# Scaling h by its root mean square on ScalarE, ahead of the last FFN block, in place of VectorE

## The chip, the cores and the metric

The kernel runs on one core of one Trainium2 chip. The metric is the device time of one execution in microseconds. Three executions of the kernel before took 677.26, 679.06 and 679.69 us; their median is 679.06. The profiled execution took 677.59 us.

## What is computed

The input x has the shape (2, 2048, 256), fp32. With `xn` the layer norm of x, the reference is

```
h   = xn + cosformer_attn(rmsnorm(xn, norm1_w))        # 16 heads, linear attention, cos and sin parts
m   = gelu(rmsnorm(h, norm2_w) @ mlp_w1 + mlp_b1) @ mlp_w2 + mlp_b2
ffn = bitlinear(relu(bitlinear(xn, w_fc) + gate * (xn @ v.T @ fast_b.T @ u.T)) ** 2, w_proj)
out = x + (h + m) + ffn
rmsnorm(h, w) = h * rsqrt(mean(h * h) + 1e-6) * w
```

The attention is causal and is written with running sums of k and v. The hidden width of both feed-forward parts is 1024. The change is about `rmsnorm(h, norm2_w)`: the multiplication of h by `rsqrt(mean(h * h) + 1e-6)`. The weight `norm2_w` is folded into `mlp_w1` when the kernel sets up.

## The kernel before

The 4096 tokens are taken in 8 tiles of 512 tokens (four blocks of 128, two of each batch). Tile 0 and tile 7 are written out, tiles 1 to 6 run in a loop. There is no planner: every engine has its own instruction stream, written by hand in the order in which it executes, and the streams meet in semaphores only. A waiting instruction holds everything that stands behind it on its engine.

In a tile TensorE does the attention of the four blocks, between them the FFN part in eight hidden blocks of 128 (`ffn_up(m)`, `ffn_down(m)`), then the output projection, then the MLP in eight hidden blocks (`mlp_up(m)`, `mlp_down(m)`) between which the transposes and the q and k products of the next tile lie. Matrix products are done in fp32r with a high and a low part, so that for every hidden block ScalarE makes the activation and a high part and VectorE the low part (`split`, L908).

The stretch of the change lies between the output projection and the MLP:

- TensorE: output projection (L1289) into two PSUM banks, `ffn_down(5)`, `ffn_up(7)` (L1143 and L1148), `ffn_down(6)` (L1158), then for each block k a wait for `hs_done` and two transposes of `xs` (L1301), then the first half of `mlp_up(0)` (L1315), which waits for `cT_hi`, then `ffn_down(7)`.
- VectorE: two adds that make h (`ctxn`, L980), `split(6)`, the scaling of the four blocks of h by `r2` into `xs` (L985), `split(7)`, then the low part of the transposed h (`cT_lo`, L990), and the read-out of the FFN sums (L996).
- ScalarE: `ffn_block(6)`, four Squares of h with a running sum (L702), which write the squares themselves into `xs` as waste, `ffn_block(7)` (Relu L646, Square L649, copy L651), the high part of the transposed h (`cT_hi`, L707), the scaling of the next tile's x into `xs` (L587), and the MLP's Gelu passes (L656, L659).
- GpSimd: for each half of the blocks an add (L531) and a pow with -0.5 (L533) that make `r2` from the sums; then `res = xb + ctxn` (L537), which waits for `split(7)`.

`hs_done` counts the scaled blocks; its waiter is TensorE at L1301. SP issues the DMAs and is not touched.

Of the kernel before, what the change touches and what calls it, by code (L numbers as in the profile page):

```python
# [31 lines left out]
ALU = mybir.AluOpType  # L32
ACT = mybir.ActivationFunctionType
# [4 lines left out]
NB = 4  # L38
# [42 lines left out]
def program(nc, x, qkv_w, qkv_b, out_w, out_b, norm1_w, norm2_w, mlp_w1, mlp_b1, mlp_w2, mlp_b2,  # L81
            fast_b, w_fc, w_proj, u, v, gate, consts, trig, out):
    with ExitStack() as ctx:
        def sb(name, shape, dt=F32):
            return ctx.enter_context(nc.sbuf_tensor(name, shape, dt))

        def sem(name):
            return ctx.enter_context(nc.semaphore(name))
# [28 lines left out]
        xs = sb("xs", [P, NB, E])  # L117
# [3 lines left out]
        ctxn = late[:, 1, :, :]  # L121
# [80 lines left out]
        r2 = sb("r2", [P, NB])  # L202
# [73 lines left out]
        r2_done = sem("r2_done")  # L276
        hs_done = sem("hs_done")
# [16 lines left out]
        def full_use(t, n):  # L294

            return 2 * KE + t * N_FULL + n

        def ffn_place(m):

            return m + min(max(m - 1, 0), NB)  # L300

        def ffn_use(t, m):
            return dense_use(t, ffn_place(m))
# [7 lines left out]
        def mlp_use(t, m, more):  # L311
            return dense_use(t, NB + mlp_place(m, more))

        def mlp_full(t, m, more):
            return full_use(t, mlp_place(m, more))
# [13 lines left out]
        def shared_use(t, n):  # L329

            return KE + t * N_SHARED + n

        def later(eng, sem_, n):

            if not isinstance(n, int) or n > 0:
                eng.wait_ge(sem_, n)

        def chunk_block(j):

            return (j % B) * 2 + j // B  # L340
# [215 lines left out]
        def _(act):  # L556
            def z_hi(t):

                act.wait_ge(upd_full, t * N_UPD + 1)
                act.activation(z_st[:, :], upd_ps[:, :], ACT.Copy).then_inc(z_hi_done, 1)  # L560
# [5 lines left out]
            def w1_hi_half(k):  # L566

                act.wait_ge(in_w1[k], 16)
                act.activation(raw_w1[k], raw_w1[k], ACT.Copy, scale=n2w[:, k:k + 1]).then_inc(w1_hi_done, 1)
                act.wait_ge(w1_hi_done, 2 * k + 1)  # L570
                act.activation(w1_hi[:, k, :], raw_w1[k], ACT.Copy).then_inc(w1_hi_done, 1)
# [11 lines left out]
            def scale_x(t):  # L583
                act.wait_ge(ln_pow, t * 8 + 7)
                act.wait_ge(x_in, t * 32 + 32)
                for k in range(NB):
                    act.activation(xs[:, k, :], xin[:, k, :], ACT.Identity, scale=xs_scale[:, k:k + 1],  # L587
                                   bias=xs_bias[:, k:k + 1]).then_inc(xs_done, 1)

            def x_hi(t):  # L590
                for m in range(KE):
                    act.wait_ge(shared_full, shared_use(t, m - KE) + 1)
                    act.activation(xT_hi[:, m, :], shared[m][:, :], ACT.Copy).then_inc(xT_hi_done, 1)

            def relu_kq(t):

                if not isinstance(t, int) or t:
                    act.wait_ge(q_trig_done, t * 2 * NB)
                for i, (dst, base) in enumerate(((kT, KE), (qT, 0))):
                    for m in range(KE):  # L600
                        act.wait_ge(dense_full, kq_full(t, i * KE + m) + 1)
                        act.activation(dst[:, m, :], dense[m][:, :], ACT.Relu,
                                       bias=qkb[:, base + m:base + m + 1]).then_inc(dense_free, 1)
# [37 lines left out]
            def body(t, more):  # L641
                def ffn_block(m):

                    act.wait_ge(dense_full, full_use(t, m) + 1)
                    later(act, wide_used, t * 2 * HB + max(m - 1, 0))
                    act.activation(wide[:, m % 2, :], dense[ffn_place(m) % 2][:, :], ACT.Relu,  # L646
                                   scale=scales[:, m:m + 1]).then_inc(dense_free, 1)
                    act.wait_ge(dense_free, ffn_use(t, m) + 1)
                    act.activation(wide[:, m % 2, :], wide[:, m % 2, :], ACT.Square).then_inc(wide_done, 1)  # L649
                    act.wait_ge(wide_done, t * HB + m + 1)  # L650
                    act.activation(wide_hi[:, m % 2, :], wide[:, m % 2, :], ACT.Copy).then_inc(hi_done, 1)  # L651

                def mlp_block(m):
                    act.wait_ge(dense_full, mlp_full(t, m, more) + 1)
                    act.wait_ge(wide_used, t * 2 * HB + HB + m - 1)
                    act.activation(wide[:, m % 2, :], dense[m % 2][:, :], ACT.Gelu_apprx_tanh,  # L656
                                   bias=b1[:, m:m + 1]).then_inc(dense_free, 1)
                    act.wait_ge(dense_free, mlp_use(t, m, more) + 1)
                    act.activation(wide_hi[:, m % 2, :], wide[:, m % 2, :], ACT.Copy).then_inc(hi_done, 1)  # L659

                def trig_v(j):

                    k = chunk_block(j)
                    act.wait_ge(shared_free, shared_use(t, S_V + k // 2) + 1)
                    later(act, upd_full, t * N_UPD + max(2 * j - 1, 0))
                    for r in range(2):
                        c = 2 * POS + 2 * r + k % 2
                        act.activation(v_trig[:, j % 2, :, r, :],
                                       v_tok[:, k, :, :].rearrange("p (m h) e -> p m (h e)", m=KE),
                                       ACT.Copy, scale=tab[:, c:c + 1]).then_inc(v_trig_done, 1)  # L670

                act.wait_ge(tab_in, t * 16 + 16)
                act.wait_ge(q_lo_stacked, (t + 1) * N_Q_LO * 16)
                trig_v(0)
                ffn_block(0)

                for g in range(2):
                    act.wait_ge(k_turned, t * 2 + g + 1)
                    act.activation(k_tok[:, 2 * g:2 * g + 2, :].rearrange("p b n -> p (b n)"), accum[g][:, :],
                                   ACT.Copy).then_inc(k_tok_done, 1)  # L680
                ffn_block(1)
                if isinstance(t, int) and t == 0:
                    w1_hi_half(1)
                def read_context(j):

                    act.wait_ge(av_done, (t * NB + j + 1) * 4)
                    later(act, ctx_full, t * NB + j)
                    act.activation(ctxT[:, :], dense[0][:, :], ACT.Copy).then_inc(dense_free, 1)  # L688

                for j in range(NB):  # L690
                    if j + 1 < NB:
                        trig_v(j + 1)
                    read_context(j)
                    ffn_block(j + 2)
                for m in range(KE):
                    act.wait_ge(shared_full, shared_use(t, S_CT + m) + 1)
                    act.activation(cT_hi[:, m, :], shared[m][:, :], ACT.Copy).then_inc(cT_hi_done, 1)
                ffn_block(6)
                for k in range(NB):

                    act.wait_ge(shared_free, shared_use(t, S_OUT + k // 2) + 1)
                    act.activation(xs[:, k, :], ctxn[:, k, :], ACT.Square, scale=float(E) ** -0.5,  # L702
                                   accum_out=mean_sq[:, k:k + 1]).then_inc(ssq_done, 1)
                ffn_block(7)
                for m in range(KE):
                    act.wait_ge(shared_full, shared_use(t, S_HT + m) + 1)
                    act.activation(cT_hi[:, m, :], shared[m][:, :], ACT.Copy).then_inc(cT_hi_done, 1)  # L707
                if more:
                    scale_x(t + 1)
                for m in range(HB):  # L710
                    mlp_block(m)
                    if m == 0 and more:
                        x_hi(t + 1)
                    if m == MLP_BEFORE_KQ - 1 and more:
                        relu_kq(t + 1)
                if more:
                    z_hi(t + 1)

            body(0, True)
            with act.Fori(1, NT - 1) as t:  # L720
                body(t, True)
            body(NT - 1, False)


        @block.vector
        def _(dve):
# [177 lines left out]
            def body(t, more):  # L904
# [75 lines left out]
                    dve.tensor_tensor(ctxn[:, 2 * g:2 * g + 2, :].rearrange("p b n -> p (b n)"), shared[g][:, :],  # L980
                                      xn[:, 2 * g:2 * g + 2, :].rearrange("p b n -> p (b n)"), ALU.add).then_inc(shared_free, 1)
                split(6)
                for k in range(NB):
                    dve.wait_ge(r2_done, t * 4 + k // 2 * 2 + 2)
                    dve.tensor_scalar(xs[:, k, :], ctxn[:, k, :], r2[:, k:k + 1], None, ALU.mult).then_inc(hs_done, 1)  # L985
                split(7)

                for m in range(KE):
# [388 lines left out]
```

## Time and profile before

| | before |
|---|---|
| median of three runs | 679.06 us |
| profiled execution | 677.59 us |
| its span | 675.6 us |
| TensorE matmul busy | 610.4 us (90%) |
| VectorE busy | 428.1 us (63%) |
| ScalarE busy | 363.6 us (54%) |
| GpSimd busy | 245.4 us (36%) |
| mean granted TensorE clock | 0.979 |

The span runs from the first to the last instruction of the profiled execution; the rest of its time lies around it. An engine's busy time is the time in which it executes instructions; matmuls are pipelined, so that their durations overlap. In the timelines PE is TensorE, PEld its weight load, DVE VectorE, ACT ScalarE and POOL GpSimd.

### The profile page before, as it was taken

How to read it: one execution, taken by the hardware profiler on the slowest of the kernel's cores; microseconds unless marked ns; L12 is line 12 of the kernel's file. 1: busy time of each engine (PE TensorE's matmuls, PEld its weight loads, DVE VectorE, ACT ScalarE, POOL GpSimd, SP SyncE). 2: the span in 40 equal slices, each digit the busy share in tenths (PEclk: the TensorE clock that was granted, in tenths of full speed). 3: DMA queues.
4: the chain of work that ended last, by engine and by line, in shares of the span. 5: the costliest groups of instructions: out<-in, count | busy, mean ns of one | idle time of the engine just before them, and what ended most of it. 6: DMA issues, size and time to landing. Idle time of an engine off the chain costs nothing.

```text
span 675.6 us, 14042 instructions
## 1 busy us (share of the span) xinstructions
PE 610.4 (90%) x4686; PEld 527.0 (78%) x4686; DVE 428.1 (63%) x829; ACT 363.6 (54%) x655; POOL 245.4 (36%) x270
## 2 busy tenths in 40 slices
PE   1559699999899999999999999999999999999987
PEld 1457587888779878898878978798878978798876
DVE  3966776567574776657665776647665675747542
ACT  2356347455664548454574548455564538455553
POOL 6315432334431543334412544324423534314130
PEclk9869799999999999999999999999999999999999
DMA  7473000640026200550016200460016300450000
GB/s 200 141 167 83 32 17 1 141 109 17 1 72 113 66 16 0 126 123 16 0 43 130 75 16 0 117 131 9 7 27 138 83 16 0 108 109 2 1 1 31
DMA packets 27991, 41.99 MB, mean 62 GB/s; under 512 B 9008, under 2 KB 19904, under 8 KB 27968
## 3 DMA queue, kind: packets, MB, share of 16 engines
q1 hardware_dynamic: 26784, 40.12, 25.9%
q10 hardware_dynamic: 1184, 1.57, 0.8%
q8 instruction: 14, 0.23, 0.2%
q14 instruction: 9, 0.07, 0.0%
HBM read 12.31 MB, written 4.19 MB: 24 GB/s over the span
## 4 chain that ended last, share of the span: by engine, by line
PE 74%; DVE 15%; ACT 5%; issue 3%; POOL 1%; DMA 0%; DVEq 0%; ACTq 0%; SPq 0%; POOLq 0%
PE accum L1158 17%; PE dense L1143 7%; PE dense L1315 7%; PE ctx_ps L1206 5%; PE dense L1193 5%; PE shared L1181 4%; PE dense L1053 4%; PE dense L1320 4%; PE shared L1067 4%; PE upd_ps L1228 3%; PE shared L1289 3%; DVE wide_lo L908 3%; PE dense L1057 2%; PE dense L1148 2%; DVE weighted L916 2%
## 5 line engine op out<-in xcount | busy, mean ns | idle before, releaser
L908 DVE TENSOR_TENSOR wide_lo<-wide,wide_hi 128x512 fp32r<-128x512 f32 x128 | 114.6, 896 | 78.4 <-ACT wide_hi L659 72.2
L916 DVE TENSOR_TENSOR weighted<-shared,cst 128x512 f32<-128x512 f32 x128 | 84.7, 682 | 27.5 <-PE shared L1181 27.5
L523 POOL TENSOR_TENSOR state<-state,added 128x272 f32<-128x272 f32 x64 | 56.1, 877 | 116.6 <-PE ctx_ps L1206 100.3
L493 POOL TENSOR_TENSOR arena<-arena,tab 128x256 f32<-128x256 f32 x64 | 49.4, 794 | 120.9 <-DMA q_stack<-arena 120.9
L656 ACT ACTIVATE wide<-dense,b 128x512 f32<-128x512 f32 x64 | 44.1, 689 | 78.9 <-PE dense L1320 78.5
L1158 PE MATMUL accum<-w_hi,wide_hi 128*128 128x256 f32 x256 | 73.2, 286 | 8.5 <-DVE wide_lo L908 8.5
L1158 PE MATMUL accum<-prT,wide_hi 128*128 128x256 f32 x256 | 72.3, 309 | 1.1 <-DVE wide_lo L908 1.1
L1158 PE MATMUL accum<-w_lo,wide_hi 128*128 128x256 f32 x256 | 71.3, 279 | 0.0
L1158 PE MATMUL accum<-w_hi,wide_lo 128*128 128x256 f32 x256 | 71.3, 278 | 0.0
L646 ACT ACTIVATE wide<-dense,scales 128x512 f32<-128x512 f32 x64 | 44.0, 688 | 47.7 <-PE dense L1148 39.7
L688 ACT ACTIVATE ctxT<-dense 128x512 f32<-128x512 f32 x32 | 19.1, 598 | 92.2 <-PE dense L1193 92.2
L1158 PE MATMUL accum<-prT,wide_lo 128*128 128x256 f32 x256 | 65.2, 282 | 0.0
L1158 PEld LDWEIGHTS accum<-w_hi,wide_hi 128*128 128x128 f32 x256 | 48.0, 188 | 16.3 <-DVE wide_lo L908 13.0
L1315 PE MATMUL dense<-cT_hi,w_hi 128*128 128x512 f32 x128 | 51.8, 405 | 6.4 <-ACT cT_hi L707 6.4
L1181 PE MATMUL shared<-q_stack,k_stack 128*128 128x256 f32 x256 | 51.8, 304 | 5.9 <-DVE weighted L916 5.9
L1143 PE MATMUL dense<-xT_hi,fcT 128*128 128x512 f32 x128 | 54.7, 428 | 0.0
L1158 PEld LDWEIGHTS accum<-prT,wide_hi 128*128 128x128 f32 x256 | 48.8, 191 | 4.7 <-DVE wide_lo L908 1.9
L1158 PEld LDWEIGHTS accum<-prT,wide_lo 128*128 128x128 f32 x256 | 48.9, 191 | 2.2
L1143 PE MATMUL dense<-xT_lo,fcT 128*128 128x512 f32 x128 | 50.2, 392 | 0.0
L1315 PE MATMUL dense<-cT_hi,w_lo 128*128 128x512 f32 x128 | 50.1, 391 | 0.0
L1158 PEld LDWEIGHTS accum<-w_lo,wide_hi 128*128 128x128 f32 x256 | 48.2, 188 | 1.7
L543 POOL TENSOR_TENSOR late<-late 128x1024 f32<-128x1024 f32 x8 | 19.2, 2395 | 83.7 <-DVE arena L781 80.1
(169 smaller groups left out, 1534.1 us busy)
## 6 DMA issues: line engine op xcount, KB each, us to landing
k_stack<-weighted SPq DMA_DIRECT2D x96, 128.0 KB, 2.6
q_stack<-arena SPq DMA_DIRECT2D x192, 64.0 KB, 2.3
xin<-L_attn_x SPq DMA_DIRECT2D x16, 256.0 KB, 2.9
out<-late SPq DMA_DIRECT2D x16, 256.0 KB, 2.3
tab<-trig SPq DMA_DIRECT2D x8, 258.0 KB, 2.7
arena<-L_ffn_w_fc SPq DMA_DIRECT2D x1, 1024.0 KB, 8.2
late<-L_ffn_w_proj SPq DMA_DIRECT2D x1, 1024.0 KB, 7.2
late<-L_attn_mlp_w ACTq DMA_DIRECT2D x1, 1024.0 KB, 5.6
```

The source lines that it names most:

```text
L493: pool.tensor_tensor(q_trig[:, j % 2, r, :, :], qT[:, :, k * P:(k + 1) * P], row.broadcast_to([P, KE, P]), ALU.mult).then_inc(q_trig_done, 1)
L523: pool.tensor_tensor(state[:, j % B, m, :], state[:, j % B, m, :], added[:, n % 2, :], ALU.add).then_inc(upd_used, 1)
L646: act.activation(wide[:, m % 2, :], dense[ffn_place(m) % 2][:, :], ACT.Relu, scale=scales[:, m:m + 1]).then_inc(dense_free, 1)
L656: act.activation(wide[:, m % 2, :], dense[m % 2][:, :], ACT.Gelu_apprx_tanh, bias=b1[:, m:m + 1]).then_inc(dense_free, 1)
L908: dve.tensor_tensor(wide_lo[:, n % 2, :], wide[:, n % 2, :], wide_hi[:, n % 2, :].bitcast(F32), ALU.subtract).then_inc(lo_done, 1)
L916: dve.tensor_tensor(weighted[:, g, :].rearrange("p (a n) -> p a n", a=4), shared[g % 2][:, :].rearrange("p (a n) -> p a n", a=4), mask.rea ...
L1143: pe.matmul(bank[:, :], fcT[:, i // 2, cols], (xT_hi, xT_lo)[i % 2][:, i // 2, :], start=(i == 0), stop=False)
L1158: mm = pe.matmul(accum[k // 2][:, (k % 2) * E:(k % 2 + 1) * E], a[:, n % 2, tok], w[:, n % HB, :], start=(first and i == 0 and k % 2 == 0) ...
L1181: mm = pe.matmul(bank[:, i * 2 * P:(i + 1) * 2 * P].rearrange("p (r n) -> p r n", r=2), k_stack[:, row, m, tok], q_stack[:, row, :, m, tok ...
L1193: mm = pe.matmul(bank[32 * i:32 * i + VW, g * P:(g + 1) * P], v_tok[:, k, h, :], weighted[:, g, i * P:(i + 1) * P], start=(g == 0), stop=True,
L1206: mm = pe.matmul(heads[:, m * (H // KE):(m + 1) * (H // KE), 0:VW], q_trig[:, j % 2, r, m, :], state[:, j % B, m, r * HW:(r + 1) * HW].rea ...
L1315: pe.matmul(bank[:, :], w[:, k, cols], cT_hi[:, k, :], start=(k == 0 and i == 0), stop=False)
```

## The change

ScalarE scales h, directly behind the four Squares and ahead of `ffn_block(7)`; it waits for the same count of `r2_done` as VectorE did, and counts the same `hs_done`. VectorE's four instructions a tile go. Nothing else is changed.

```diff
@@ ScalarE, body(t) @@
                     act.wait_ge(shared_free, shared_use(t, S_OUT + k // 2) + 1)
                     act.activation(xs[:, k, :], ctxn[:, k, :], ACT.Square, scale=float(E) ** -0.5,
                                    accum_out=mean_sq[:, k:k + 1]).then_inc(ssq_done, 1)
+                for k in range(NB):
+                    act.wait_ge(r2_done, t * 4 + k // 2 * 2 + 2)
+                    act.activation(xs[:, k, :], ctxn[:, k, :], ACT.Copy, scale=r2[:, k:k + 1]).then_inc(hs_done, 1)
                 ffn_block(7)
@@ VectorE, body(t) @@
                 split(6)
-                for k in range(NB):
-                    dve.wait_ge(r2_done, t * 4 + k // 2 * 2 + 2)
-                    dve.tensor_scalar(xs[:, k, :], ctxn[:, k, :], r2[:, k:k + 1], None, ALU.mult).then_inc(hs_done, 1)
                 split(7)
```

## Rows read from the trace of the kernel before

**Rows 1.** The page: busy time of each engine; shares of the chain by engine.
```profile
PE 610.4 (90%) x4686; PEld 527.0 (78%) x4686; DVE 428.1 (63%) x829; ACT 363.6 (54%) x655; POOL 245.4 (36%) x270
...
PE 74%; DVE 15%; ACT 5%; issue 3%; POOL 1%; DMA 0%; DVEq 0%; ACTq 0%; SPq 0%; POOLq 0%
```

**Rows 2.** Waits of TensorE: us in total, times, longest us.
```profile
PE accum L1158 <- DVE wide_lo L908: 9.6, 11, 1.2
...
PE dense L1315 <- ACT cT_hi L707: 6.4, 8, 0.9
```

**Rows 3.** The chain of waits, tile 3: start us, us, what.
```profile
337.04 0.25 PE dense L1148
...
337.39 0.70 ACT wide L646
...
339.35 0.56 ACT cT_hi L707
...
339.95 1.22 PE dense L1315 x4
```

**Rows 4.** Timeline of ScalarE: start us, us, instruction, count, idle before.
```profile
304.01 0.92 ACT L668 ACTIVATE arena<-arena,tab 128x272 f32<-128x272 f32 x2
...
336.40 0.40 ACT L702 ACTIVATE xs<-late 128x256 f32<-128x256 f32 x1
336.71 0.19 ACT L702 ACTIVATION_READ_ACCUMULATOR xs<-late 128x1 f32 x1
...
338.78 0.63 ACT L651 ACTIVATE wide_hi<-wide 128x512 fp32r<-128x512 f32 x1
...
340.27 2.07 ACT L587 ACTIVATE xs<-xin,xs_bias,xs_scale 128x256 f32<-128x256 f32 x4
```

**Rows 5.** Timelines of VectorE, GpSimd and TensorE, tile 3.
```profile
335.87 0.68 DVE L908 TENSOR_TENSOR wide_lo<-wide,wide_hi 128x512 fp32r<-128x512 f32 x1
...
338.08 0.62 DVE L985 TENSOR_SCALAR xs<-late,r 128x256 f32<-128x256 f32 x2 [0.33 <-POOL r L533]
339.44 0.69 DVE L908 TENSOR_TENSOR wide_lo<-wide,wide_hi 128x512 fp32r<-128x512 f32 x1 [0.74 <-ACT wide_hi L651]
...
335.89 1.22 POOL L533 TENSOR_TENSOR r<-ms,half 128x2 f32<-128x2 f32 x1
...
337.35 0.70 POOL L533 TENSOR_TENSOR r<-ms,half 128x2 f32<-128x2 f32 x1
...
338.04 1.15 PE L1301 MATMUL shared<-cst,xs 128*128 128x128 f32 x8
```

**Rows 6.** Timelines of GpSimd and ScalarE, tiles 2 and 7.
```profile
260.63 0.70 POOL L533 TENSOR_TENSOR r<-ms,half 128x2 f32<-128x2 f32 x1
...
260.77 0.69 ACT L646 ACTIVATE wide<-dense,scales 128x512 f32<-128x512 f32 x1 [0.55 <-PE dense L1148]
...
643.07 0.69 ACT L646 ACTIVATE wide<-dense,scales 128x512 f32<-128x512 f32 x1 [0.42 <-PE dense L1148]
643.11 0.70 POOL L533 TENSOR_TENSOR r<-ms,half 128x2 f32<-128x2 f32 x1
```

**Rows 7.** Groups of instructions: busy us, mean ns | idle before.
```profile
L668 ACT ACTIVATE arena<-arena,tab 128x272 f32<-128x272 f32 x64 | 29.6, 509 | 11.5 <-DVE arena L800 11.5
...
L985 DVE TENSOR_SCALAR xs<-late,r 128x256 f32<-128x256 f32 x32 | 9.9, 350 | 7.2 <-POOL r L533 7.2
```

**Rows 8.** TensorE's timeline, then stretches with busy times and granted clock (PEclk).
```profile
72.98 0.80 PE L1181 MATMUL shared<-q_stack,k_stack 128*128 128x256 f32 x2 [5.87 <-DVE weighted L916]
...
73.00:76.00 3.00, 3.00 (x12) 2.77 (x13) 2.23 (x6) 0.00 (x0) 1.54 (x3) 0.50 0.00 0
76.00:80.00 4.00, 4.00 (x48) 3.49 (x47) 1.73 (x3) 0.00 (x0) 0.98 (x2) 0.77 0.01 4
```

**Rows 9.** Groups of instructions again: the low parts and GpSimd's add.
```profile
L908 DVE TENSOR_TENSOR wide_lo<-wide,wide_hi 128x512 fp32r<-128x512 f32 x128 | 114.6, 896 | 78.4 <-ACT wide_hi L659 72.2 <-ACT wide_hi L651 6.1
...
L543 POOL TENSOR_TENSOR late<-late 128x1024 f32<-128x1024 f32 x8 | 19.2, 2395 | 83.7 <-DVE arena L781 80.1 <-DVE wide_lo L908 3.5
```

## The prediction

> **What bounds the kernel now.** I read the page's busy shares first, then its chain of waits, then the list of who waited for whom, and last the timelines of the five engines around the edited lines. TensorE is busy 90% of the span and holds 74% of the chain that ended last; ScalarE is busy 54%, VectorE 63% [rows 1]. So both engines that the change touches have idle time, and shares alone would say that four small instructions may move between them at no price. The wait list says otherwise for this place: TensorE waits 8 times, once a tile, for ScalarE's `cT_hi` (L707) ahead of the first MLP matmul (L1315), 6.4 us in all [rows 2]. The chain shows what stands behind that wait, and the reader is to see that it runs through ScalarE without a hole: the last matmul of FFN block 7 (L1148), ScalarE's Relu of that block at 337.39, its Square, the copy, then `cT_hi`, and TensorE starts again at 339.95 [rows 3]. ScalarE is the least busy of the three here on average, and yet is the one that the path goes through in this stretch.
>
> **The change, part by part.** The numbers below are from the tile at 330 to 345 us (tile 3); the others follow.
>
> *Removed from VectorE:* four `tensor_scalar` on L985, 0.35 us each, 32 in the program, 9.9 us busy [rows 7]. The last pair of a tile runs from 338.08 to 338.70 [rows 5], ahead of a gap of VectorE: the next thing it does, the split of block 7 (L908, 339.44), waits for ScalarE's copy L651, not for VectorE [rows 5]. So the removal is worth nothing by itself: 0 us. What they feed are the transposes L1301. TensorE arrives there at 338.04, when it has finished with FFN block 6, and is through at 338.04 + 1.15 = 339.19 [rows 5]. ScalarE's `cT_hi` starts at 339.35 [rows 3], right behind the copy L651, which ends at 338.78 + 0.63 = 339.41 [rows 4] (consecutive ScalarE instructions overlap a little). Scaled rows of h that were ready earlier would therefore bring at most 0.1 us, since ScalarE itself is not free before.
>
> *Added to ScalarE:* four copies with a per-partition scale, between the last Square (its accumulator read ends at 336.71 + 0.19 = 336.90) and the Relu of block 7 (337.39) [rows 3, 4]. ScalarE executes in the order written, so everything behind the copies waits for them: the three passes of block 7, both `cT_hi`, and behind these the scaling of the next x (L587).
>
> *The added wait:* copies 0 and 1 wait for the first pow on GpSimd, which ends at 335.89 + 1.22 = 337.11; copies 2 and 3 for the second, 337.35 + 0.70 = 338.05 [rows 5]. A VectorE instruction starts 0.03 behind such an end (338.08, [rows 5]); I take 0.04 for ScalarE.
>
> *The price of one copy:* the nearest row is L668, the same Copy with a scale by pointer, SBUF to SBUF, 128x272: 0.51 us each [rows 7], and the two of a pair take 0.92 together [rows 4], so the second starts 0.92 - 0.51 = 0.41 behind the first. The bounds from both sides: 0.31 from start to accumulator read for the Square of the same 256 columns without a pointer (336.40 to 336.71), and 2.07 / 4 = 0.52 for L587, 256 columns with two pointers [rows 4]. I take 0.41, the row nearest in form.
>
> *The sum for a tile:* copies 0 and 1 run from 337.15 to 337.97, that is inside ScalarE's present idle time and inside GpSimd's second pow; they cost nothing. Copy 2 starts at 338.05 + 0.04 = 338.09, copy 3 at 338.50, the Relu of block 7 at 338.91 in place of 337.39: 1.52 later. Behind it nothing on ScalarE has slack until L1315, so TensorE starts there at 341.47 in place of 339.95. The cover that hid the pow and the scaling until now was block 7's own work on ScalarE (2.0 us, 337.39 to 339.41); the change takes the cover away, since the two now stand one behind the other.
>
> *Over the tiles:* only the distance between the end of the second pow and the present start of the Relu differs. It is 0.66 in tile 3. In three of the eight tiles (2, 5, 6) it is near that of tile 2: 260.63 + 0.70 - 260.77 = 0.56; in the last it is 643.11 + 0.70 - 643.07 = 0.74 [rows 6]; tiles 0, 1 and 4 are like tile 3 (0.65 to 0.68). The eight add up to 5.07. To each come 0.04 + 2 x 0.41 = 0.86, 6.9 in all. The sum is +12.0 us.
>
> *Is it given back behind L1315?* FFN block 7 down (L1158), cT_lo, the res add L537 on GpSimd, the accumulator read-out L996 and the whole MLP stage all start from instructions that are moved by the same 1.5 us. TensorE has no wait for a DMA in the loop that could swallow it: its waits are for VectorE and ScalarE [rows 2]. I take no recovery.
>
> *The skill's view.* VectorE does the multiply in 0.35 us, ScalarE's nearest form takes 0.51 [rows 7]. The Trainium skill (ScalarE: Activation LUTs, Rules for kernel authors) puts plain multiplications on VectorE and not on ScalarE. By durations alone that rule would make the change cost 32 x 0.14 = 4.5 us, since the same page (What ACT_TABLE_LOAD costs) gives 186 ns + 0.833 ns per element + 93 ns for a pointer, an estimate of 0.49 us for 256 columns. The trace agrees with the direction of the rule, but the sum by ScalarE's queue is more than twice as large, because it holds the wait for GpSimd's pow and the whole length of two copies, not the difference in length between two engines.
>
> **Bounds.** With 0.31 a copy: 5.07 + 8 x 0.66 = +10.4. With 0.52 and a wake-up of 0.10: 5.07 + 8 x 1.14 = +14.2. Even copies of no duration would cost 5.07 + 0.3 = 5.4, because the second pow ends after the Relu's present start.
>
> **Reference.** The profiled execution took 677.59 us (span 675.6 and 1.99 around it); the median of the runs shown, 679.06, is 1.47 higher. The sum gives 677.59 + 12.0 = 689.6 on the profile's own time and 691.0 on the median. I state 690.2, between them. Its own range is 677.59 + 10.4 = 688.0 to 679.06 + 14.2 = 693.3.
>
> **Rivals.**
> (a) *Not slower: the delay is taken back in the MLP stage.* VectorE's split L908 takes 0.90 on average [rows 9] where an undisturbed one takes 0.69 [rows 5]; GpSimd's adds of 2.4 us (L543 and, behind it, L465) run beside the long ones [rows 9]. TensorE's waits for L908 add up to 9.6 us [rows 2]. If the 1.5 us moved VectorE's splits against GpSimd's adds so that they no longer meet, up to 9.6 would come back: 677.6 + 12.0 - 9.6 = 680.0, which is within 0.5% of before (0.5% is 3.4 us, about what a measurement of this kernel tells from no change). It decides where L543 starts earlier against the splits than now. Against it: L543 waits for VectorE's own q parts (L781) in 80.1 us of its idle time [rows 9], and those are behind the same delay, so both move together. The Trainium skill (GPSIMD Engine Reference, Specifications) says that GpSimd shares its SBUF interfaces with VectorE, in contention with VectorE instructions of two SBUF inputs; the stretched splits agree.
> (b) *Slower than forecast: the clock falls.* TensorE's hole in front of L1315 grows from 339.95 - 339.19 = 0.76 [rows 3, 5] to some 2.0 us. Behind the hole of 5.87 us in the first tile the granted clock was 0.50 from 73 to 76 and 0.77 from 76 to 80, so it came back at about 78, and work from 72.98 on ran 4.9 us at 1.2 in place of 2.4 GHz: 2.4 us lost [rows 8]. Eight times that gives 689.6 + 19.6 = 709. Against it: holes of up to 1.2 us stand in every tile today [rows 2] with a mean granted clock of 0.979 over the span, its setup included, and the new hole is nearer to those than to 5.87.
> (c) *A smaller price:* if the removed VectorE work let GpSimd's pows run sooner (the first of tile 3 takes 1.22, the second 0.70), the second could not end before the last Square's 336.90 + 0.70 = 337.60, 0.45 ahead of now; eight times that is 3.6, and the time on the profile's own 689.6 - 3.6 = 686.0. For it: the second pow starts only when the first is through. Against it: the long pow stands beside the split L908 at 335.87 [rows 5], which stays, and not beside L985.
> That the change doesn't do what it says is excluded: the order on each engine is the written one.
>
> **Chances.** Forecast 0.83, (a) 0.06, (b) 0.04, (c) 0.04, something unseen 0.03. From them: slower by over 0.5% 0.93, within 0.5% 0.05, faster by over 0.5% 0.02. Range 686.5 to 694.5: the forecast's own, widened by 1.5 below, which takes in most of (c), and 1.2 above for the spread of the runs.
>
> **What the profile after would show.** Right: a new ScalarE group of 32 copies at about 0.5 us, 16 us busy in all; VectorE busy down by 9.9; idle time of ScalarE before the copies put down to GpSimd's pow; Relu of block 7 about 0.85 behind the second pow's end in each tile; TensorE's waits on ScalarE at L1315 and L1301 together up from 6.4 to about 18; the clock 1.00 behind tile 0. Wrong: the Relu of block 7 still starting with L1148's end; or L1315 1.5 us later but the stage behind it shorter by as much (a); or clock below 1.00 in the loop (b).

## The result, and the profile after

The changed kernel takes 693.98 us (median of four runs, 693.13 to 694.92) against 678.16 before (675.71 to 679.69). The ratio is 1.0237, interval 1.0201 to 1.0273: slower by 15.8 us. The profiled execution took 693.6 us, its span 691.6 against 675.6, 16.0 more. The forecast of 690.2 (range 686.5 to 694.5) has the right sign and holds the time, but the sum of 12.0 us is short by 4.

The busy shares of the kernel after say as little as those of before [rows 1]. The reader is to see that VectorE's time fell by 7.3 us, that ScalarE's rose by 13.2, and that TensorE, whose instructions are the same, is busy 6.7 us longer: something makes its own work slower. VectorE's fell by less than the 9.9 us of the four instructions that are gone, because two groups of the setup (the split of the second MLP weight) took 11.6 us in this execution and 8.8 in that of before; with seven matmuls in the hole (below), which leaves VectorE as the change does, it is busy 417.3 us.

```profile
PE 617.1 (89%) x4686; PEld 532.0 (77%) x4686; DVE 420.8 (61%) x797; ACT 376.8 (54%) x687; POOL 244.2 (35%) x270
```

The waits of the kernel after, us in total, times, longest, answer to [rows 2]. TensorE's wait for `cT_hi` (now L710) grows from 6.4 to 15.7 us; its wait for VectorE's low parts stays (9.0 against 9.6); and ScalarE waits eight times for the pow.

```profile
PE dense L1315 <- ACT cT_hi L710: 15.7, 8, 2.0
...
PE accum L1158 <- DVE wide_lo L911: 9.0, 11, 1.0
...
ACT xs L706 <- POOL r L533: 2.1, 8, 0.3
```

The timelines of GpSimd, ScalarE and TensorE after, tile 3, answer to [rows 3 to 5].

```profile
342.03 0.70 POOL L533 TENSOR_TENSOR r<-ms,half 128x2 f32<-128x2 f32 x1
...
343.44 0.70 POOL L533 TENSOR_TENSOR r<-ms,half 128x2 f32<-128x2 f32 x1
...
342.90 0.19 ACT L702 ACTIVATION_READ_ACCUMULATOR xs<-late 128x1 f32 x1
342.99 0.90 ACT L706 ACTIVATE xs<-late,r 128x256 f32<-128x256 f32 x2
344.17 0.91 ACT L706 ACTIVATE xs<-late,r 128x256 f32<-128x256 f32 x2 [0.28 <-POOL r L533]
344.98 0.67 ACT L646 ACTIVATE wide<-dense,scales 128x512 f32<-128x512 f32 x1
...
346.88 1.07 ACT L710 ACTIVATE cT_hi<-shared 128x512 fp32r<-128x512 f32 x2
...
343.13 0.39 PE L1148 MATMUL dense<-z_st,gT 128*128 128x512 f32 x1
...
344.29 1.27 PE L1301 MATMUL shared<-cst,xs 128*128 128x128 f32 x8
347.51 0.50 PE L1315 MATMUL dense<-cT_hi,w_hi 128*128 128x512 f32 x1 [1.94 <-ACT cT_hi L710]
```

The second pow ends at 343.44 + 0.70 = 344.14, copies 2 and 3 start at 344.17, the Relu of FFN block 7 at 344.98: 0.84 behind the pow. It used to start at once behind the last matmul of its block; now that matmul starts at 343.13 and the Relu 1.85 later. The same matmul and L1315 before, tile 3:

```profile
336.88 0.40 PE L1148 MATMUL dense<-z_st,gT 128*128 128x512 f32 x1
...
339.95 0.50 PE L1315 MATMUL dense<-cT_hi,w_hi 128*128 128x512 f32 x1 [0.76 <-ACT cT_hi L707]
```

From L1148 to L1315 it was 3.07 us and is 4.38. Of the 1.31 more, 1.18 is the longer hole; the rest lies in the transposes L1301, which now wait for the copies (1.27 against 1.15 in all).

What the sum did not hold is in the granted clock. These are stretches of the kernel after, with the busy times of the five engines and, third from the end, the clock of TensorE: the stretch behind the long hole in tile 3, then those in tiles 5 and 7.

```profile
348.00:352.00 4.00, 4.00 (x27) 3.40 (x26) 2.55 (x6) 3.63 (x8) 2.26 (x1) 1.00 0.00 0
...
502.00:506.00 4.00, 2.32 (x7) 1.93 (x8) 1.89 (x3) 3.97 (x8) 1.97 (x1) 0.70 0.00 0
506.00:510.00 4.00, 4.00 (x24) 3.52 (x24) 1.89 (x5) 2.14 (x5) 0.41 (x1) 0.87 0.00 0
...
658.00:662.00 4.00, 1.97 (x6) 1.46 (x7) 1.89 (x3) 2.71 (x5) 1.34 (x1) 0.83 0.00 0
662.00:666.00 4.00, 3.94 (x17) 3.15 (x16) 1.69 (x5) 1.34 (x3) 1.02 (x1) 0.74 0.00 0
```

The start of L1315 in successive tiles turns this into time. Before, tiles 3 and 4 start it at 339.95 and 416.64, 76.69 apart. After, these are the starts of tiles 3 to 6:

```profile
347.51 0.50 PE L1315 MATMUL dense<-cT_hi,w_hi 128*128 128x512 f32 x1 [1.94 <-ACT cT_hi L710]
...
425.61 0.50 PE L1315 MATMUL dense<-cT_hi,w_hi 128*128 128x512 f32 x1 [1.94 <-ACT cT_hi L710]
...
503.68 0.80 PE L1315 MATMUL dense<-cT_hi,w_hi 128*128 128x512 f32 x1 [1.94 <-ACT cT_hi L710]
...
583.31 0.50 PE L1315 MATMUL dense<-cT_hi,w_hi 128*128 128x512 f32 x1 [1.94 <-ACT cT_hi L710]
```

The distances are 78.10, 78.07 and 79.63. A tile without a fall of the clock costs 1.4 us more than before; tile 5, whose matmul behind the hole takes 0.80 in place of 0.50, costs another 1.5. The same hole of 1.94 us stands ahead of both kinds. Tile 7 has a fall too, and from its L1315 to the end it is 31.17 against 29.89, 1.3 more. Tile 0 also has a fall (0.64 from 110 to 114).

The whole 16.0 us of the two profiled executions falls into three parts. Up to L1148 of block 7 in tile 0 it is 105.64 against 103.70 us, 1.9 more. The change touches nothing there, and in a second execution the difference is gone (below). The eight stretches from L1148 to L1315, where the change lies, last 35.7 against 24.5 us together, 11.1 more. All that stands behind L1315 in the eight tiles, where the falls are, lasts 550.3 against 547.4, 3.0 more.

### The profile page after: what moved, and what is told of

Read it like the earlier page. It is cut to its first block and busy times, and to the rows that moved or that the text cites. A ratio compares the mean times of both kernels' runs of the same rounds, so it can differ in the third digit from the quotient of the medians.

```text
span 691.6 us, 14042 instructions
## 1 busy us (share of the span) xinstructions
PE 617.1 (89%) x4686; PEld 532.0 (77%) x4686; DVE 420.8 (61%) x797; ACT 376.8 (54%) x687; POOL 244.2 (35%) x270
## 5 line engine op out<-in xcount | busy, mean ns | idle before, releaser
L1158 PE MATMUL accum<-w_hi,wide_hi 128*128 128x256 f32 x256 | 73.2, 286 | 8.2 <-DVE wide_lo L911 8.2
L1158 PE MATMUL accum<-prT,wide_hi 128*128 128x256 f32 x256 | 74.5, 316 | 0.8 <-DVE wide_lo L911 0.8
L1158 PE MATMUL accum<-w_lo,wide_hi 128*128 128x256 f32 x256 | 71.4, 279 | 0.0
L1158 PE MATMUL accum<-w_hi,wide_lo 128*128 128x256 f32 x256 | 71.4, 279 | 0.0
L1158 PE MATMUL accum<-prT,wide_lo 128*128 128x256 f32 x256 | 67.2, 288 | 0.0
L1315 PE MATMUL dense<-cT_hi,w_hi 128*128 128x512 f32 x128 | 52.8, 413 | 15.7 <-ACT cT_hi L710 15.7
L1158 PEld LDWEIGHTS accum<-w_hi,wide_hi 128*128 128x128 f32 x256 | 48.1, 188 | 15.8 <-DVE wide_lo L911 12.8
L1181 PE MATMUL shared<-q_stack,k_stack 128*128 128x256 f32 x256 | 52.2, 306 | 2.5 <-DVE weighted L919 1.8
L1158 PEld LDWEIGHTS accum<-prT,wide_hi 128*128 128x128 f32 x256 | 50.5, 197 | 4.0 <-DVE wide_lo L911 1.6
L1158 PEld LDWEIGHTS accum<-prT,wide_lo 128*128 128x128 f32 x256 | 50.6, 198 | 2.4
L1315 PE MATMUL dense<-cT_hi,w_lo 128*128 128x512 f32 x128 | 51.3, 401 | 0.0
L1158 PEld LDWEIGHTS accum<-w_lo,wide_hi 128*128 128x128 f32 x256 | 48.2, 188 | 1.7
```

Of the source, the lines that this page charges most:

```text
L1158: mm = pe.matmul(accum[k // 2][:, (k % 2) * E:(k % 2 + 1) * E], a[:, n % 2, tok], w[:, n % HB, :], start=(first and i == 0 and k % 2 == 0) ...
L1181: mm = pe.matmul(bank[:, i * 2 * P:(i + 1) * 2 * P].rearrange("p (r n) -> p r n", r=2), k_stack[:, row, m, tok], q_stack[:, row, :, m, tok ...
L1315: pe.matmul(bank[:, :], w[:, k, cols], cT_hi[:, k, :], start=(k == 0 and i == 0), stop=False)
```

## The experiments

"Distance" is that of the L1315 starts of tiles 3 and 4, read as above, "falls" is the number of tiles in which the clock fell behind the changed stretch, both of the profiled execution; "hole" is TensorE's idle time right before L1315. In the kernel with the copies behind block 7 another hole of 1.74 stands before the transposes. Four kernels were timed on the chip where before takes 678.11 us and four where it takes 677.43; times of two kernels are compared within one chip, or by what each lies above before there.

| kernel | median us | of before, same chip | ratio, interval | distance | hole | falls |
|---|---|---|---|---|---|---|
| before | | 678.16 | | 76.69 | 0.76 to 0.85 | 0 |
| changed | 693.98 | 678.16 | 1.0237 (1.0201 to 1.0273) | 78.10 | 1.94 to 2.04 | 3 |
| changed, again | 692.21 | 678.11 | 1.0212 (1.0163 to 1.0262) | 78.12 | 1.94 to 2.03 | 4 |
| the wait alone | 684.55 | 678.11 | 1.0089 (1.0059 to 1.0118) | 77.59 | 1.53 to 1.59 | 0 |
| copies that don't wait | 688.13 | 678.11 | 1.0169 (1.0113 to 1.0226) | 77.77 | 1.79 to 1.94 | 3 |
| changed, 7 matmuls in the hole | 688.13 | 678.11 | 1.0146 (1.0103 to 1.0188) | 78.14 | 0.33 to 0.42 | 0 |
| changed, 3 matmuls in the hole | 688.13 | 677.43 | 1.0168 (1.0143 to 1.0192) | 78.09 | 1.25 to 1.34 | 0 |
| blocks 0, 1 on ScalarE | 681.23 | 677.43 | 1.0057 (1.0040 to 1.0074) | 76.91 | 0.97 to 1.31 | 0 |
| copies behind block 7 | 699.86 | 677.43 | 1.0330 (1.0293 to 1.0368) | 78.77 | 0.58 to 0.67 | 4 |
| before, filler in the setup hole | 676.71 | 677.43 | 0.9994 (0.9971 to 1.0016) | 76.80 | 0.76 to 0.85 | 0 |

The profiled executions in the three parts of above, us: the start of L1148 in tile 0, the eight stretches from L1148 to L1315, and the rest of the span.

| kernel | start | stretches | rest | span |
|---|---|---|---|---|
| before | 103.7 | 24.5 | 547.4 | 675.6 |
| changed | 105.6 | 35.7 | 550.3 | 691.6 |
| changed, again | 102.8 | 36.0 | 551.9 | 690.7 |
| the wait alone | 105.9 | 30.7 | 547.7 | 684.3 |
| copies that don't wait | 102.5 | 32.4 | 551.4 | 686.2 |
| changed, 7 matmuls in the hole | 104.0 | 36.0 | 546.6 | 686.6 |
| changed, 3 matmuls in the hole | 103.2 | 36.2 | 546.2 | 685.6 |
| blocks 0, 1 on ScalarE | 103.6 | 28.1 | 546.5 | 678.2 |
| copies behind block 7 | 104.4 | 41.6 | 551.3 | 697.2 |
| before, filler in the setup hole | 101.8 | 24.6 | 546.4 | 672.7 |

The start varies without an order. The stretches follow ScalarE's queue, and the rest is long in the four profiles that have falls and in no other.

**The changed kernel once more.** No edit.

> The changed kernel once more, beside the others on one chip. Theory A (the copies and the wait for GpSimd's second pow stand on ScalarE ahead of FFN block 7, about 1.4 us a tile on the path) gives 11 to 12 us over the kernel before. Theory B (behind the longer hole of TensorE, 1.94 us, the granted clock falls in some tiles, about 1.3 us each time) gives the rest, 2 to 4 us; if B holds, a second profile shows such falls too, perhaps in other tiles, and if the falls of the first profile were a disturbance of that execution, it shows none and the difference is near 12. Rival C (the setup is slower by 1.9 us because of the change) expects the first L1315 wait of tile 0 again near 110.2 us against 106.8; if that part is the spread of executions, it moves.

Theory A and B both stand: 14.1 us slower, and in tiles 3 to 6 distances of 78.12, 79.59 and 78.12. The falls are now in tiles 0, 1, 4 and 7, where those of the first profile were in 0, 5 and 7. These stretches of the second profile are tile 4's, which had no fall in the first:

```profile
422.00:426.00 4.00, 2.06 (x7) 1.43 (x8) 1.75 (x3) 3.94 (x8) 0.90 (x1) 0.84 0.00 0
426.00:430.00 4.00, 4.00 (x22) 3.62 (x22) 1.61 (x5) 2.14 (x5) 1.49 (x1) 0.74 0.00 0
```

Rival C falls: L1315 of tile 0 starts at 107.38 here, not at 110.2. Over the ten profiles it starts between 104.84 and 110.21, with no order by the change, so the 2 us ahead of the change are the spread of executions.

**The wait alone.** In the kernel before:

```diff
+                act.wait_ge(r2_done, t * 4 + 4)
                 ffn_block(7)
```

> The kernel before, with VectorE scaling as before, but ScalarE waits for the second pow ahead of FFN block 7. Theory A: the Relu starts 0.04 behind the pow's end, 0.56 to 0.74 + 0.04 later than before in a tile, 5.4 us in all; no or few falls of the clock. The rival that only ScalarE's longer duration costs (4.5 us for 32 copies) expects no change here.

6.4 us slower, where a price by ScalarE's longer durations alone would show nothing. The distance grows by 0.90, a little over the forecast 0.7, because the Relu starts 0.18 behind the pow and not 0.04; two more waits stand in its queue between the added one and the Relu, which may be the reason; no run shows it. The timelines of its GpSimd and ScalarE, tile 3:

```profile
341.87 0.70 POOL L533 TENSOR_TENSOR r<-ms,half 128x2 f32<-128x2 f32 x1
...
342.75 0.69 ACT L646 ACTIVATE wide<-dense,scales 128x512 f32<-128x512 f32 x1 [1.34 <-PE accum L1159]
```

The bracket names a matmul group as the releaser; the added wait is for the pow, which ends at 342.57; of three waits in a row the bracket names one.

**Copies that don't wait.** In the changed kernel:

```diff
-                    act.wait_ge(r2_done, t * 4 + k // 2 * 2 + 2)
-                    act.activation(xs[:, k, :], ctxn[:, k, :], ACT.Copy, scale=r2[:, k:k + 1]).then_inc(hs_done, 1)
+                    act.wait_ge(ssq_done, t * NB + k + 1)
+                    act.activation(xs[:, k, :], ctxn[:, k, :], ACT.Copy, scale=ones[:, k:k + 1]).then_inc(hs_done, 1)
```

> The changed kernel, but the four copies take their scale from a column of ones that is there from the start, so they don't wait for GpSimd (h is not divided by its root mean square). Theory A: four copies of 0.40 from the last Square on, so the Relu starts about 1.0 us later than before, 8 to 8.5 us in all, and 3 us less than the changed kernel without its clock falls. If the wait were the whole price, this would be near the kernel before; if only the difference of the durations counted, +4.5.

This kernel leaves out the division of h by its root mean square, so it shows times only. 10.0 us slower. The distance grows by 1.08, 8.6 us over eight tiles, as expected; three falls of the clock come on top, which the expectation had not counted on. The stretches grow by 6.2 us with the wait alone and by 7.8 with the copies alone, together 14.0, but by 11.1 and 11.5 with the change: copies 0 and 1 run during the wait. This is the overlap that the sum had put in (copies 0 and 1 at nothing).

**A filled hole.** In the changed kernel, behind the transposes L1301; with `range(3)` in the second kernel:

```diff
+                for i in range(7):
+                    pe.matmul(ctx_ps[:, :], fcT[:, 0, 0:P], xT_hi[:, 0, :], start=True, stop=True)
```

> The changed kernel with seven matmuls of 512 columns in TensorE's hole between the transposes L1301 and L1315, 7 x 0.23 = 1.6 us of 1.94, into a PSUM bank that nothing reads. Theory B: the clock stays at 1.00 in the loop, the waits stay on ScalarE, and the time is 2 to 3 us below the changed kernel. Rival: the falls have another cause or cost nothing, and the time is that of the changed kernel or up to 1 us above it.

> The changed kernel with three matmuls in place of seven in the hole ahead of L1315, which leaves TensorE idle there for about 1.25 us. Theory B, if holes of that length are harmless as those of 1.5 to 1.6 us in the kernel with the wait alone: no falls in the loop and the time of the kernel with seven, 688. If any shortening less than a full cover leaves the falls, 690 to 692.

Both take 688.13 us, though TensorE does more work. With seven matmuls that is 4.1 us below the changed kernel on the same chip and 10.0 above before; with three, on another chip, it is 10.7 above before (one of its four runs took 690.64). The changed kernel is 14.1 and 15.8 above before. The distances are those of the changed kernel in its tiles without falls (78.14 and 78.09), so the filler costs nothing, and ScalarE's queue is as long as in the changed kernel. There are no falls in the eight tiles, and the rest behind L1315 is 3.7 to 5.7 us shorter than in the changed kernel's two profiles. TensorE's timeline of tile 3 with seven matmuls, then the stretch of that tile, and the stretches of tile 7, where the changed kernel has 0.83 and 0.74:

```profile
342.62 1.86 PE L1305 MATMUL ctx_ps<-xT_hi,fcT 128*128 128x512 f32 x7
344.81 0.50 PE L1317 MATMUL dense<-cT_hi,w_hi 128*128 128x512 f32 x1 [0.33 <-ACT cT_hi L710]
```

```profile
342.00:346.00 4.00, 3.67 (x18) 2.51 (x17) 1.69 (x3) 3.94 (x8) 0.83 (x1) 1.00 0.00 0
654.00:658.00 4.00, 3.58 (x18) 2.73 (x19) 1.89 (x3) 2.71 (x5) 1.34 (x1) 1.00 0.00 0
658.00:662.00 4.00, 2.81 (x17) 2.16 (x16) 2.46 (x6) 2.64 (x4) 1.05 (x1) 1.00 0.00 0
```

Theory B is shown by this pair: with the same order on ScalarE and the same stretches, the falls go when TensorE has something to do in the hole, and the time goes down. It does not rest on the profiled executions alone: over all eight runs of the changed kernel the mean granted clock is 0.968 to 0.975, over the eight with a filler 0.979 to 0.982, and over the 22 of before on the two chips 0.977 to 0.982.

**Half the copies.** In the changed kernel ScalarE's loop runs over `range(2)`, and VectorE does blocks 2 and 3 as before:

```diff
                 split(6)
+                dve.wait_ge(hs_done, t * NB + 2)
+                for k in range(2, NB):
+                    dve.wait_ge(r2_done, t * 4 + k // 2 * 2 + 2)
+                    dve.tensor_scalar(xs[:, k, :], ctxn[:, k, :], r2[:, k:k + 1], None, ALU.mult).then_inc(hs_done, 1)
                 split(7)
```

> ScalarE scales blocks 0 and 1 only, blocks 2 and 3 stay on VectorE. Theory A: ScalarE no longer waits for the second pow; its two copies end the Relu's present idle time and push it by 0.2 us where the first pow is short and by 0.57 where it is long, 2 to 4.5 us over the kernel before in all, and no falls of the clock, since TensorE's hole stays under 1.4 us. A rival by count (half the copies, half the price) expects +6 to +8.

3.8 us slower, 0.57% with an interval of 0.40 to 0.74: far below half the price. ScalarE no longer waits for the second pow, and its two copies fall in part into what was its idle time ahead of the Relu: the eight stretches grow by 3.5 us, 0.1 to 0.6 in a tile. The Relu of tile 3 starts here at 338.38, while the second pow is still running (337.77 + 0.70 = 338.47).

**Copies behind block 7.** In the changed kernel the loop is moved behind `ffn_block(7)`.

> All four copies on ScalarE, but behind FFN block 7. Theory A: the pow's wait is covered again by block 7, but the transposes now start only with the copies, so cT_hi comes at 339.32 + 4 x 0.40 + transposes, about 2.0 us later than before in a tile, 16 us in all, plus the clock falls: 694 to 701. If the place of the wait were all that matters, it would be near the kernel with copies that don't wait, +8 to +10.

22.4 us slower, at the upper end. The distance grows by 2.08, 16.6 over eight tiles, as expected, and four falls come on top. The pow is covered by block 7 again, but the transposes now wait for copies that stand behind the block. Its TensorE, tile 3:

```profile
348.44 1.55 PE L1301 MATMUL shared<-cst,xs 128*128 128x128 f32 x8 [1.74 <-ACT xs L707]
350.56 0.51 PE L1315 MATMUL dense<-cT_hi,w_hi 128*128 128x512 f32 x1 [0.58 <-ACT cT_hi L710]
```

**The setup hole of the kernel before.** In tile 0, behind `turn_context(0)`:

```diff
+                    if isinstance(t, int) and t == 0 and j == 0:
+                        for i in range(22):
+                            pe.matmul(dense[0][:, :], fcT[:, 0, 0:P], xT_hi[:, 0, :], start=True, stop=True)
```

> The kernel before with 22 matmuls of 512 columns, some 5 us, in TensorE's hole of 5.9 us in tile 0, where the clock stood at half for about 5 us behind it. Theory B: without that fall 2 to 2.5 us are saved (676). If the filler lies where TensorE isn't waiting, or the hole comes elsewhere in some executions, it costs up to 5 us instead.

No change in the median (0.9994, interval 0.9971 to 1.0016), but its ten runs lie in two groups, five from 674.07 to 675.35 and five from 678.06 to 679.47, with nothing between, where the thirteen of before run from 676.19 to 678.61. The profiled one is of the lower group, and its clock stays at 1.00 where that of before was 0.62 and 0.52:

```profile
70.00:74.00 4.00, 2.97 (x16) 2.18 (x14) 3.94 (x8) 0.00 (x0) 1.96 (x3) 1.00 0.43 131
74.00:78.00 4.00, 4.00 (x52) 3.52 (x54) 3.26 (x7) 0.00 (x0) 1.98 (x4) 1.00 0.00 0
```

In that execution the filler does what theory B says. A likely reason for the upper group is that the setup comes in two forms. The hole stands before L1181 in five of the other nine profiles (5.87 us in that of before, [rows 8]) and before L1193 in four, among them both of the changed kernel. In the first of these it is 4.75 us:

```profile
68.72 0.63 PE L1193 MATMUL dense<-weighted,arena 128*17 128x128 f32 x8 [4.75 <-DVE weighted L919]
```

The filler would then stand where TensorE isn't waiting; no profile of the upper group shows it. Over its ten runs this kernel is no faster, and none of the others beats the one before.

## Why the prediction was right, and where its sum was short

- *ScalarE is on the path here though its busy share is low:* right. It rests on the chain, and the wait alone, one semaphore wait and no work, costs 6.4 us.
- *VectorE's four instructions are worth nothing:* not tried apart from the rest. VectorE's idle time before block 7's split rose to 34.3 us in eight waits; the tile grew by what ScalarE's queue explains.
- *The copies' pace:* forecast 0.41 from start to start; in tile 3 the second pair starts at 344.17 and the Relu at 344.98, 0.405 each. The group has 32 copies of 0.50 us, against 0.51 in the nearest row:

```profile
L706 ACT ACTIVATE xs<-late,r 128x256 f32<-128x256 f32 x32 | 14.5, 499 | 2.2 <-POOL r L533 2.1
```

- *Copies 0 and 1 free, then pow, then two copies:* right. The Relu stands 0.84 or 0.85 behind the second pow in every tile of both profiles, against 0.86 in the sum. The stretches grew by 11.1 and 11.5 us, 1.39 and 1.43 a tile against 1.50 on average.
- *Rival (c), a shorter first pow through the change:* it falls. The first pow is short (0.70) in three tiles before, in five and in three of the two profiles of the changed kernel. Its length goes with its start beside VectorE's split, which stays, and not with L985. Before, it is short in tile 2, where it starts 0.03 ahead of the split, and takes 1.22 in tile 3, where it starts 0.02 behind [rows 5]:

```profile
259.16 0.70 POOL L533 TENSOR_TENSOR r<-ms,half 128x2 f32<-128x2 f32 x1
...
259.19 0.70 DVE L908 TENSOR_TENSOR wide_lo<-wide,wide_hi 128x512 fp32r<-128x512 f32 x1
```

- *No recovery behind L1315:* right within 1 us. The rest of the span is 547.4 us before and 546.6 and 546.2 in the two kernels with a filler, which have the changed order and no falls. TensorE's waits for the low parts changed by 0.6 us. Rival (a), which wanted 9.6, falls.
- *The clock:* this is the term that failed. The sum put it at nothing, and rival (b) was given 4 in 100, because the new hole of 2.0 us was judged nearer to the harmless ones of up to 1.2 us than to the 5.87 us one. (Holes of 1.2 didn't stand in every tile either: the one of 1.22 stands in the last tile alone, and the others of L1158 are at most 0.96.) The runs showed (b) to be half true: the clock fell in 3 tiles of one profile and in 4 of the other, and a fall costs 1.5 us in tiles 4 and 5, not 2.4. Behind L1315 the changed kernel is 3.0 and 4.5 us longer than before, 3.7 to 5.7 longer than with a filler, and filling the hole takes 4.1 us off its time on the same chip.
- *Why the forecast still held:* in part by luck. The queue was put 0.5 to 0.9 us too high and the clock 3.0 to 4.5 too low, and 693.98 lies 0.5 below the upper end of the range. That end was made of a copy of 0.52, a wake-up of 0.10 and the spread of the runs. The copy came at 0.405 and the wake-up at 0.03 (344.17 behind 344.14), and the room that these left took in the clock.
- *The durations:* the Trainium skill (ScalarE: Activation LUTs, Rules for kernel authors) had the sign right in putting a multiplication on VectorE; the price by durations that the prediction took from that page, an estimate of 4.5 us, is under a third of the 14.1 and 15.8 measured. The wait alone costs 6.4 us and adds no instruction that counts as busy.

Of the signs that the prediction named, TensorE's waits came to 15.7 us and not 18, since part of the price lies in the longer transposes, and the clock was not 1.00 behind tile 0.

What stays open: why one tile with a hole of 1.94 us is followed by a fall and the next is not, in one execution. The hole is the same to 0.01 us. The stretch ahead of it is 0.16 longer where the first pow is long, but that doesn't decide: in the second profile tiles 5 and 6 have the long form (4.54 and 4.55) and no fall, and tile 1 has the short one (4.38) and a fall.

## What to carry to other kernels

Before moving an instruction to an engine with idle time, follow the chain at that very place: put the moved instructions, with what they wait for, into the queue of the new engine and shift everything behind them. A wait ahead of path work costs as much as work: here the wait alone came to 6.4 us where the whole change costs 14.1. When a sum adds a hole on TensorE, add the clock to it: a hole need not be long to be followed by a fall in some of its passes, and a filler of useless matmuls in the hole is a cheap experiment that separates the two.

## What the runs showed of the hardware

- Behind a hole of 1.94 to 2.04 us of TensorE the granted clock fell to the lower of its two levels, 1.2 GHz, in some tiles and stayed at 2.4 GHz in others: 3 and 4 of 8 tiles in two profiles of one kernel, 3 of 8 in the kernel with copies that don't wait (1.79 to 1.94), 4 of 8 in that with the copies behind block 7 (1.74, the transposes, then 0.58 to 0.67), none in the six other profiles of the table.
- With matmuls in that hole that left 0.33 to 0.42 or 1.25 to 1.34 us of it, the clock fell in none of 16 tiles, and in none of 8 behind holes of 1.53 to 1.59 us (the wait alone).
- The matmul that starts at the lower level takes 0.80 us for 512 columns (503.68) where it takes 0.50 in the tiles without a fall, and a fall costs 1.5 us in tiles 4 and 5 (79.63 against 78.10 and 78.07, 79.59 against 78.12) and 1.6 in tile 1 (80.67 against 79.03). In tile 0 it hardly shows: the distance to tile 1 is 80.19 and 80.42 with a fall, and 79.49 and 79.99 in the kernels with seven and three matmuls in the hole, which have none.
- GpSimd's pow of 128x2 takes 1.15 to 1.22 us or 0.69 to 0.70, by its start beside VectorE's split of 128x512 next to it. In the ten profiles all 80 first pows follow this: the long ones start 0.01 to 0.09 us behind the split, the short ones 0.03 or 0.04 ahead of it.
- The setup varies by itself: L1315 of tile 0 starts anywhere from 104.84 to 110.21 us, and the clock's fall there lasts 3 to 14 us in nine profiles. A difference of 2 us between two single profiles of this kernel says nothing until the tiles are compared one by one.
